# One transformer layer with expert choice: the output projection split in two halves, root refinement and scaling one pair later, row sums behind the masks in the last batch

## The chip, the core and the metric

One core of one Trainium2 chip. The metric is the device time of one execution in microseconds; of the kernel before it was measured three times, and the median counts. One further execution was taken with the hardware profiler. Matrix products run on TensorE (PE; its weight loads are PEld), elementwise work and reductions on VectorE (DVE), activations and copies on ScalarE (ACT), some elementwise work on GpSimd (POOL); SyncE (SP) issues most transfers.

## The reference, cut to what matters

The input is x, 16 batches of 256 rows of 256 numbers, and a condition per batch. All is float32.

```
h   = layernorm(x) * g + b + (silu(cond) @ W_ada.T + b_ada)
qkv = h @ Wqkv.T                       # 16 heads of 64
q,k = layernorm over each head of 64, times gain, plus bias
o   = softmax(q @ k.T / 8) @ v         # per batch and head
x   = x + o @ Wout.T                   # the output projection
gate = softmax(x @ Wgate.T)            # 8 experts
each expert takes its 512 best tokens of all 4096: layernorm, two linear
layers with gelu between, times the gate value, added to the token's row
```

## The kernel before

**Entries and steps.** The attention part runs through `over_batches` (L172): an entry −1 that prepares, entries 0 to 15, one per batch, and an entry 16 that finishes. Entries 2 to 13 are a hardware loop, the others are written out. `cur`, `nxt` and `prv` say whether the entry attends its own batch, projects q, k and v of the next, and finishes the one before. An entry has eight steps (`hp`), one per pair of heads, and every engine has its own in-order program of them, tied by semaphores. Behind the entries the experts are chosen and run (`phase23_*`), which the change touches in one count.

**One step on TensorE** (L1381 on), in this order: transposes of q and k of the next pair (L1398, into `pq`); a chunk of q, k or v for the coming group of pairs (`chunk`, six matmuls of 512 columns, lines L488 to L490 of the helper `three_passes`); the product of probabilities and V of the pair before (L1420, into `av`); that pair's row sums (`ones` times `prob_sum`, L1424, also into `av`); the masks, which write minus the row maximum into `sc` (L1436); the scores of this pair (L1445); rough scores of the next pair for its row maximum (L1458, into `mx`); a second chunk. Steps 2 and 6 have no chunks. The masks need the row maxima `m`, the scores also the low half `qk_lo`.

**What the others do in a step.** ScalarE evacuates the transposes (L1060 to L1066), takes logarithm and exponential of the row sums for their inverse (L1087, L1089), then the exponential of the scores (L1093), then the high half of the divided output (`o_hi`, L1098). GpSimd adds the two halves of the probabilities (`prob_sum`, L980), makes `qk_lo` (L987) and the low half `o_lo` (L992). VectorE divides (three instructions, L1250 to L1254), sums squares of the chunks (L1215) and takes the maxima (L1269), in that order. PE's product of a pair waits for the division of the pair before (`divided`).

**Scaling of q and k.** For each group of four pairs the inverse roots are guessed on ScalarE (`power_guess`, L1006), refined by four small operations on GpSimd (`refine`, L941) and applied on VectorE (`normalise`, L1180, four `times_rstd` of 128x512, L894). For the group of pairs 4 to 7 all three stand in step 0 (in entry 0 `refine` stands in step 1, ahead of `qk_lo`).

**Output projection.** Step 0 of an entry ends with the whole projection of the batch before: 2 row tiles by 8 pairs by 3 passes, 48 matmuls of 256 columns (L1475 on). It waits for `o_lo` of pairs 0 to 6, and in the first tile for that of pair 7 just before it is used. In step 1 VectorE subtracts the result from the residual row `xr_sb` into `tok` (L1233; the division leaves its result with the sign turned), in step 2 it takes statistics of `tok`, in step 3 those of the next input; in step 6 PE transposes `tok` and forms the gate's logits.

**Banks.** Chunks, projection, transposes and logits alternate between the two PSUM banks `ch`. `batch_slots` lists who uses one in each entry and who reads it, `make_counts` derives parity and the wait that frees the bank two uses later:

```
        if prv:
            out += [(0, 2, "wout", "dve"), (6, 0, "tokT", "act"), (6, 1, "gate", "dve")]
```

**SyncE** stores `tok` and reloads `xr_sb` when VectorE has read the projection.

## Time and profile before

| | us |
|---|---|
| median of 3 runs | 1189.99 |
| lowest, highest | 1188.55, 1192.36 |
| the profiled execution, its own time | 1187.28 |
| its span, first to last instruction | 1185.4 |
| PE busy in the span | 1089.6 |

Two microseconds of the profiled execution lie around its span. In the profile "busy" is the time in which an engine works at something; for PE the ends are modelled, so the distance from one matmul's start to the next is the better measure of its pace. An idle time is put down to what ended it. Attention takes the span to about 901 us, the choice of tokens goes to about 983 us, the experts take the rest.

### The profile page before, as it was taken

The page shows a single profiled execution, that of the slowest core. Times are in us where ns is not written, and L with a number is a line of the kernel's source. Part 1 is how long each engine was busy: PE and PEld are TensorE (multiplying, and loading weights), DVE is VectorE, ACT ScalarE, POOL GpSimd, SP SyncE. Part 2 cuts the span into 40 slices and gives each one's busy share as a digit, 9 for nine tenths or more (in the row PEclk, how much of TensorE's full clock was granted, in tenths as well). Part 3 has the DMA queues.
Part 4 walks back from the last instruction along what each step waited for, and adds up shares of the span by engine and source line. Part 5 has one row for each costly group of instructions (what it writes and reads, how often), then busy time and mean ns, then how long its engine had stood idle before and what let it go on. Part 6 is the DMA issues. An engine that isn't in the chain of part 4 may idle for free.

```text
span 1185.4 us, 24714 instructions
## 1 busy us (share of the span) xinstructions
PE 1089.6 (92%) x8379; PEld 844.3 (71%) x8379; DVE 794.8 (67%) x1620; ACT 773.8 (65%) x1460; POOL 555.3 (47%) x597
## 2 busy tenths in 40 slices
PE   6899999999999999999999999999994138999996
PEld 6667777777777777777777777777753037989995
DVE  5686667666675767666666757676655885777773
ACT  5787877868687878778687878787772104445541
POOL 2454545546464545455464645454561003454332
PEclk9999999999999999999999999999997557999998
DMA  4000000010100000000101000000004212554322
GB/s 177 19 10 19 19 19 19 18 35 0 35 18 18 18 18 18 18 18 18 35 0 35 18 18 18 18 9 19 11 19 160 50 36 92 150 153 126 107 27 28
DMA packets 31774, 48.62 MB, mean 41 GB/s; under 512 B 7920, under 2 KB 28528, under 8 KB 30448
## 3 DMA queue, kind: packets, MB, share of 16 engines
q1 hardware_dynamic: 25584, 39.49, 10.2%
q0 software_dynamic: 6144, 8.52, 4.0%
q8 instruction: 28, 0.46, 0.2%
q14 instruction: 18, 0.15, 0.0%
HBM read 35.29 MB, written 12.71 MB: 40 GB/s over the span
## 4 chain that ended last, share of the span: by engine, by line
PE 86%; DVE 7%; issue 2%; POOL 2%; ACT 2%; DMA 1%; SPq 0%; DVEq 0%; POOLq 0%; ACTq 0%
PE ch L488 14%; PE ch L490 12%; PE ch L489 12%; PE av L1420 10%; PE sc L1445 9%; PE sc L1436 6%; PE pq L1398 5%; PE av L1424 5%; PE mx L1458 2%; DVE hit L765 2%; PE sc L488 1%; PE sc L490 1%; PE sc L489 1%; PE ch L1472 1%; PE ch L1378 1%
## 5 line engine op out<-in xcount | busy, mean ns | idle before, releaser
L987 POOL TENSOR_TENSOR qk_lo<-qkT,qk_hi 128x512 fp32r<-128x512 f32 x128 | 169.8, 1327 | 259.7 <-ACT qk_hi L1066 236.6
L980 POOL TENSOR_TENSOR prob_sum<-prob 128x512 f32<-128x512 f32 x128 | 165.0, 1289 | 81.7 <-ACT prob L1093 81.4
L1250 DVE TENSOR_TENSOR av<-av,rec 128x256 f32<-128x256 f32 x128 | 55.2, 431 | 205.9 <-ACT rec L1089 200.9
L488 PE MATMUL ch<-w_hi,hT_lo 128*128 128x512 f32 x384 | 170.5, 444 | 1.0 <-DVE hT_lo L1243 1.0
L1093 ACT ACTIVATE prob<-sc 128x1024 f32<-128x1024 f32 x128 | 130.8, 1022 | 38.2 <-PE sc L1445 38.2
L1269 DVE TENSOR_REDUCE m<-mx 128x4 bf16<-128x1024 f32 x128 | 155.6, 1216 | 0.0
L490 PE MATMUL ch<-w_hi,hT_hi 128*128 128x512 f32 x384 | 151.7, 395 | 0.0
L489 PE MATMUL ch<-w_lo,hT_hi 128*128 128x512 f32 x384 | 151.5, 395 | 0.0
L1420 PE MATMUL av<-prob,V 128*64 128x256 f32 x1024 | 139.6, 394 | 6.3 <-DVE oT L1254 4.3
L894 DVE TENSOR_TENSOR qn<-raw,rstd 128x512 f32<-128x512 f32 x128 | 118.1, 981 | 32.6 <-POOL rstd L956 32.6
L992 POOL TENSOR_TENSOR o_lo<-oT,o_hi 128x256 fp32r<-128x256 f32 x128 | 100.6, 786 | 26.1 <-ACT o_hi L1098 26.1
L1420 PEld LDWEIGHTS av<-prob,V 128*64 128x64 f32 x1024 | 62.6, 136 | 64.5 <-issue 43.1
L1060 ACT ACTIVATE qkT<-pq,vec 128x256 f32<-128x256 f32 x128 | 71.7, 560 | 54.5 <-PE pq L1398 54.5
L590 POOL DMA_INDIRECT out<-yout,index x32 | 52.3, 1633 | 104.5 <-DVE yout L887 98.1
L641 ACT ACTIVATE yT<-ch,b_sb 128x512 f32<-128x512 f32 x62 | 42.6, 688 | 89.4 <-PE ch L490 80.1
L1215 DVE TENSOR_REDUCE ssum<-sq 128x8 f32<-128x512 f32 x128 | 87.1, 681 | 15.6 <-ACT sq L1045 13.8
L488 PEld LDWEIGHTS ch<-w_hi,hT_lo 128*128 128x128 f32 x384 | 72.2, 188 | 22.9 <-DVE hT_lo L1243 1.2
L1066 ACT ACTIVATE qk_hi<-qkT 128x512 fp32r<-128x512 f32 x128 | 80.7, 630 | 11.6
L1043 ACT ACTIVATE raw<-ch 128x512 f32<-128x512 f32 x128 | 75.1, 587 | 16.8 <-PE ch L490 15.9
L1445 PE MATMUL sc<-qk_hi,qk_lo 64*128 64x256 f32 x512 | 85.6, 330 | 0.0
L490 PEld LDWEIGHTS ch<-w_hi,hT_hi 128*128 128x128 f32 x384 | 72.3, 188 | 18.0
L1424 PE MATMUL av<-prob_sum,ones 128*64 128x256 f32 x512 | 77.8, 382 | 1.9 <-POOL prob_sum L980 1.9
(214 smaller groups left out, 2797.3 us busy)
## 6 DMA issues: line engine op xcount, KB each, us to landing
fcw<-experts SPq DMA_DIRECT2D x8, 2048.0 KB
x_sb<-x SPq DMA_DIRECT2D x16, 256.0 KB, 2.7
xr_sb<-x SPq DMA_DIRECT2D x16, 256.0 KB, 2.7
out<-tok SPq DMA_DIRECT2D x16, 256.0 KB, 2.2
rows_dram<-xh SPq DMA_DIRECT2D x16, 256.0 KB, 2.2
prob<-w_qk SPq DMA_DIRECT2D x2, 512.0 KB, 6.8
qn<-w_qk SPq DMA_DIRECT2D x2, 512.0 KB, 7.2
V<-w_vT SPq DMA_DIRECT2D x2, 512.0 KB, 7.3
```

Of the source, the lines that this page charges most:

```text
L488: nc.tensor.matmul(psum, l_lo, r_hi, start=first, stop=False)
L489: nc.tensor.matmul(psum, l_hi, r_lo, start=False, stop=False)
L490: return nc.tensor.matmul(psum, l_hi, r_hi, start=False, stop=last)
L894: return nc.vector.tensor_tensor(qn[par][:, c, :].rearrange("p (h d) -> p h d", d=HD), raw[:, c, :].rearrange("p (h d) -> p h d", d=HD), r ...
L980: nc.gpsimd.tensor_tensor(prob_sum[(hp - 1) % 2][:, :, :], pr[:, :, 0, :], pr[:, :, 1, :], ALU.add).then_inc(prob_summed, 1)
L987: nc.gpsimd.tensor_tensor(qk_lo[par][:, :], qkT[par][:, :], qk_hi[par][:, :].bitcast(F32), ALU.subtract).then_inc(lo_ready, 1)
L992: nc.gpsimd.tensor_tensor(o_lo[:, pair, :], oT[pair % 2][:, :], o_hi[:, pair, :].bitcast(F32), ALU.subtract).then_inc(o_split, 1)
L1093: nc.scalar.activation(prob[hp % 2][:, :], sc[:, :], ACT.Exp, scale=HD ** -0.5).then_inc(prob_ready, 1)
L1269: nc.vector.tensor_reduce(m[(hp + 1) % 2][:, :], mx[:, :].rearrange("p (a j) -> p a j", a=4), AX.X, ALU.max).then_inc(max_ready, 1)
L1420: nc.tensor.matmul(av[hh * HD:(hh + 1) * HD, 0:N], V[gpar][:, jt, i * P + hh * HD:i * P + (hh + 1) * HD], prob[(hp - 1) % 2][:, at:at + N] ...
L1424: ins = nc.tensor.matmul(av[hh * HD:(hh + 1) * HD, N:2 * N], ones[:, :], prob_sum[(hp - 1) % 2][:, hh, :], start=True, stop=True)
L1445: ins = nc.tensor.matmul(sc[:, at:at + N], k_part[par][rows, keys], q_part[par][rows, 0:N], start=False, stop=(k_part is qk_hi and q_part ...
```

## The change

The projection is made in two halves. Pairs 0 to 3 of a batch are projected at the end of step 6 of its own entry, and VectorE subtracts the result from `xr_sb` in place at the start of step 7. Pairs 4 to 7 are projected at the end of step 2 of the next entry, and VectorE makes `tok` from that at the start of step 3. Both row statistics of VectorE now stand at the end of step 3. The logits share the bank of the transposed `tok`, so that an entry still has sixteen uses of a bank. `power_guess`, `refine` and `normalise` of pairs 4 to 7 move from step 0 to step 1, `refine` behind `qk_lo`. In entry 15, steps 3 to 7, the row sums stand behind the masks. Entry 0 has a first half and no second, entry 16 a second and no first.

```diff
--- before.py
+++ after.py
@@ -68,7 +68,9 @@
     cur, nxt, prv = 0 <= b < B, b + 1 < B, 1 <= b <= B
     out = [(hp, pos, name, "act") for (hp, pos), (name, _) in CHUNKS.items() if (cur if hp < 2 else nxt)]
     if prv:
-out += [(0, 2, "wout", "dve"), (6, 0, "tokT", "act"), (6, 1, "gate", "dve")]
+out += [(2, 0, "wout_second", "dve"), (6, 0, "tokT", "act"), (6, 1, "gate", "dve")]
+    if cur:
+out += [(6, 2, "wout_first", "dve")]
     if nxt:
 out += [(1, 2, "xT", "act")]
     return sorted(out)
@@ -89,7 +91,10 @@
     key = (hp, pos)
     hit("slot", b, key)
     hit(who, b, key)
-    slots.append((b, key, who))
+    if name == "gate":
+        slots[-1] = (b, (6, 0), who, key)
+    else:
+        slots.append((b, key, who, key))
     if name in ("q", "k"):
         hit("chunk", b, key)
 for hp, live in ((0, cur or b < 0), (4, nxt or prv)):
@@ -98,12 +103,11 @@
 for kind, live in (("x_loaded", nxt), ("xr_loaded", cur), ("tok_stored", prv)):
     if live:
         hit(kind, b, 0)
-    for n, (b, key, who) in enumerate(slots):
-table["bank", b, key] = n % 2
-table["index", b, key] = n
+    for n, (b, key, who, last) in enumerate(slots):
+table["bank", b, key] = table["bank", b, last] = n % 2
 if n >= 2:
-    pb, pkey, pwho = slots[n - 2]
-    table["free", b, key] = (pwho, table[pwho, pb, pkey])
+    pb, _, pwho, plast = slots[n - 2]
+    table["free", b, key] = (pwho, table[pwho, pb, plast])
     return table
@@ -738,7 +742,7 @@
-    dve.wait_ge(dve_read, 2 * B)
+    dve.wait_ge(dve_read, 3 * B)
@@ -903,7 +907,7 @@
             sp.dma_start(x_sb[:, :, :], x[bass.ds(b + 2, 1)].rearrange("o (t p) d -> p (o t) d", p=P)
                          if not isinstance(b, int) else x[b + 2].rearrange("(t p) d -> p t d", p=P)).then_inc(x_in, 16)
         if prv:
-            need(dve_read, through("dve", b, (0, 2)))
+            need(dve_read, through("dve", b, (2, 0)))
@@ -978,8 +982,6 @@
...
-            if isinstance(b, int) and b == 0 and hp == 1:
-                refine(b, 0)
             if (cur and nxt) or (cur and hp < UNITS - 1) or (nxt and hp == UNITS - 1):
                 need(hi_ready, u + 2)
@@ -990,7 +992,7 @@
...
-            if hp == 0 and cur and not (isinstance(b, int) and b == 0):
+            if hp == 1 and cur:
                 refine(b, 0)
             if hp == 5 and (nxt or prv) and not (isinstance(b, int) and b == B):
                 refine(b, 4)
@@ -1071,6 +1073,8 @@
                 value_weights_high()
             if isinstance(b, int) and b < 0 and hp == 5:
                 weights_high(1, 0)
+            if hp == 1 and cur:
+                power_guess(b, 0)
             if hp == 5 and (nxt or prv) and not (isinstance(b, int) and b == B):
                 power_guess(b, 4)
             if isinstance(b, int) and b < 0 and hp == 5:
@@ -1094,12 +1098,12 @@
             if (cur and hp > 0) or (hp == 0 and prv):
                 need(divided, u)
                 if hp == 1 and prv:
-                    need(slot_filled, through("slot", b, (0, 2)))
+                    need(slot_filled, through("slot", b - 1, (6, 2)))
+                if hp == 5 and prv:
+                    need(slot_filled, through("slot", b, (2, 0)))
             if live:
                 chunk(b, hp, 1)
-            if hp == 0 and cur:
-                power_guess(b, 0)
             if hp == 1 and nxt:
                 need(slot_filled, through("slot", b, (1, 2)))
@@ -1221,17 +1225,23 @@
     need(rstd_ready, 1)
     input_rows(rstd[1])
+    def flat_rows(t):
+        return t[:, :, :].rearrange("p t d -> p (t d)")
+
     def batch(b, cur, nxt, prv):
         last_entry = isinstance(b, int) and b == B
         for hp in range(UNITS):
             u = b * UNITS + hp
-            if hp == 1 and prv:
-                need(slot_filled, through("slot", b, (0, 2)))
-                need(xr_in, b * 16)
+            if hp == 3 and prv:
+                need(slot_filled, through("slot", b, (2, 0)))
+                need(dve_read, through("dve", b - 1, (6, 2)))
                 need(tok_out, (b - 1) * 16)
                 need(xh2_ready, b - 1)
-                nc.vector.tensor_tensor(tok[:, :, :].rearrange("p t d -> p (t d)"), xr_sb[:, :, :].rearrange("p t d -> p (t d)"),
-                                        ch[slot_bank(b, (0, 2))][:, :], ALU.subtract).then_inc(dve_read, 1)
+                nc.vector.tensor_tensor(flat_rows(tok), flat_rows(xr_sb), ch[slot_bank(b, (2, 0))][:, :], ALU.subtract).then_inc(dve_read, 1)
+            if hp == 7 and cur:
+                need(slot_filled, through("slot", b, (6, 2)))
+                need(xr_in, (b + 1) * 16)
+                nc.vector.tensor_tensor(flat_rows(xr_sb), flat_rows(xr_sb), ch[slot_bank(b, (6, 2))][:, :], ALU.subtract).then_inc(dve_read, 1)
@@ -1252,9 +1262,6 @@
-            if hp == 3 and has_second(b):
-                need(x_in, (b + 3) * 16)
-                row_stats(x_sb, 0)
             if hp in (0, 3, 4, 7) and (cur if hp < 2 else nxt):
                 head_sums(b, hp, 0)
             if hp == 6 and prv:
@@ -1284,13 +1291,15 @@
                 else:
                     need(slot_filled, through("slot", -1, (1, 2)))
                 input_rows(rstd[0])
-            if hp == 2 and prv and not last_entry:
-
-                need(dve_read, through("dve", b, (0, 2)))
-                row_stats(tok, 2)
-            if hp == 2 and last_entry:
-                need(dve_read, through("dve", b, (0, 2)))
-                last_stats()
+            if hp == 3 and has_second(b):
+                need(x_in, (b + 3) * 16)
+                row_stats(x_sb, 0)
+            if hp == 3 and prv:
+                need(dve_read, through("dve", b, (2, 0)))
+                if last_entry:
+                    last_stats()
+                else:
+                    row_stats(tok, 2)
             if (hp == 0 and cur) or (hp == 4 and (nxt or prv) and not last_entry):
                 need(rstd_ready, through("newton", b, hp) - 1)
@@ -1300,7 +1309,7 @@
                     need(chunk_summed, through("chunk", b, (hp, 1)))
-            if hp == 0 and cur:
+            if hp == 1 and cur:
                 normalise(b, 0)
             if isinstance(b, int) and b == 0:
                 split_wout(hp)
@@ -1371,6 +1380,22 @@
                                w_hi[:, c, col:col + GW], w_lo[:, c, col:col + GW], c == 0, c == DC - 1)
         ins.then_inc(slot_filled, 1)
+    def project(bank, pairs):
+
+        for t in range(TT):
+            for pair in pairs:
+                ins = three_passes(bank[:, t * D:(t + 1) * D], o_hi[:, pair, t * P:(t + 1) * P], o_lo[:, pair, t * P:(t + 1) * P],
+                                   wo_hi[:, pair, :], wo_lo[:, pair, :], pair % GU == 0, pair % GU == GU - 1)
+        ins.then_inc(slot_filled, 1)
+
+    def row_sums(u, hp):
+
+        need(prob_summed, u)
+        for hh in range(2):
+            ins = nc.tensor.matmul(av[hh * HD:(hh + 1) * HD, N:2 * N], ones[:, :], prob_sum[(hp - 1) % 2][:, hh, :],
+                                   start=True, stop=True)
+        ins.then_inc(attended, 1)
+
@@ -1383,6 +1408,7 @@
             u = b * UNITS + hp
             ahead = (cur and nxt) or (cur and hp < UNITS - 1) or (nxt and hp == UNITS - 1)
             npar = (hp + 1) % 2
+            bare = cur and not nxt and hp > 2
             if isinstance(b, int) and b < 0 and hp == 2:
                 centre_weights(0, 1)
             if isinstance(b, int) and b < 0 and hp == 5:
@@ -1401,7 +1427,7 @@
                 chunk(b, hp, 0)
             if hp == 6 and prv:
                 bank = take_bank(b, (6, 0))
-                need(dve_read, through("dve", b, (0, 2)))
+                need(dve_read, through("dve", b, (2, 0)))
                 transposed(bank, tok)
             if (cur and hp > 0) or (hp == 0 and prv):
@@ -1419,11 +1445,8 @@
...
-                need(prob_summed, u)
-                for hh in range(2):
-                    ins = nc.tensor.matmul(av[hh * HD:(hh + 1) * HD, N:2 * N], ones[:, :], prob_sum[(hp - 1) % 2][:, hh, :],
-                                           start=True, stop=True)
-                ins.then_inc(attended, 1)
+                if not bare:
+                    row_sums(u, hp)
             if cur:
                 need(prob_ready, u)
@@ -1436,6 +1459,8 @@
...
+                if bare:
+                    row_sums(u, hp)
                 for jt in range(TT):
                     keys = slice(N + jt * P, N + (jt + 1) * P)
@@ -1465,25 +1490,25 @@
                 need(xh_ready, b + 2)
                 transposed(bank, xh)
             if hp == 6 and prv:
-                bank = take_bank(b, (6, 1))
+                bank = ch[slot_bank(b, (6, 1))]
                 need(act_read, through("act", b, (6, 0)))
...
-            if hp == 0 and prv:
-                bank = take_bank(b, (0, 2))
-                need(o_split, u - 1)
+            if hp == 2 and prv:
+                bank = take_bank(b, (2, 0))
+                need(o_split, u - 2)
                 if isinstance(b, int) and b == 1:
                     need(wo_ready, 2 * UNITS)
-                for t in range(TT):
-                    for pair in range(UNITS):
-                        if t == 0 and pair == UNITS - 1:
-                            need(o_split, u)
-                        ins = three_passes(bank[:, t * D:(t + 1) * D], o_hi[:, pair, t * P:(t + 1) * P], o_lo[:, pair, t * P:(t + 1) * P],
-                                           wo_hi[:, pair, :], wo_lo[:, pair, :], pair == 0, pair == UNITS - 1)
-                ins.then_inc(slot_filled, 1)
+                project(bank, range(GU, UNITS))
+            if hp == 6 and cur:
+                bank = take_bank(b, (6, 2))
+                need(o_split, u - 2)
+                if isinstance(b, int) and b == 0:
+                    need(wo_ready, UNITS)
+                project(bank, range(GU))
     over_batches(pe, batch)
     phase23_tensor(pe)
```

(Indentation is cut by eight columns.)

## Rows read from the trace of the kernel before

**Rows 1.** The page: TensorE's granted clock, in tenths, in 40 slices of the span.

```profile
PEclk9999999999999999999999999999997557999998
```

**Rows 2.** Windows by engine: stretch, length, busy us (instructions) per engine, granted clock, DMA.

```profile
48.40:51.70 3.30, 3.30 (x16) 1.69 (x16) 2.73 (x5) 3.21 (x8) 0.00 (x0) 0.55 0.00 0
80.00:134.40 54.40, 54.40 (x428) 40.62 (x426) 37.10 (x76) 42.62 (x87) 28.78 (x33) 1.00 0.06 16
```

**Rows 3.** Timeline of entry 0, steps 1 to 5: start, length, instruction, [idle before].

```profile
41.73 4.66 DVE L894 TENSOR_TENSOR qn<-raw,rstd 128x512 f32<-128x512 f32 x4 [1.90 <-POOL rstd L956]
...
42.78 0.42 ACT L1089 ACTIVATE rec<-log_sum 128x256 f32<-128x256 f32 x1
...
44.54 0.60 PE L1398 MATMUL pq<-con,qn 128*128 128x128 f32 x4
...
46.97 0.42 DVE L1250 TENSOR_TENSOR av<-av,rec 128x256 f32<-128x256 f32 x1
...
48.40 1.98 PE L1420 MATMUL av<-prob,V 128*64 128x256 f32 x8 [3.26 <-DVE oT L1254]
...
50.59 0.69 DVE L1243 TENSOR_TENSOR hT_lo<-hT,hT_hi 128x512 fp32r<-128x512 f32 x1
...
53.33 0.48 PE L488 MATMUL ch<-w_hi,hT_lo 128*128 128x512 f32 x1
...
73.08 2.83 DVE L894 TENSOR_TENSOR qn<-raw,rstd 128x512 f32<-128x512 f32 x4
```

**Rows 4.** Timeline of a middle entry, step 0: around the output projection.

```profile
580.04 0.74 POOL L992 TENSOR_TENSOR o_lo<-oT,o_hi 128x256 fp32r<-128x256 f32 x1 [1.56 <-ACT o_hi L1098]
580.08 0.28 PE L488 MATMUL ch<-wo_hi,o_lo 128*128 128x256 f32 x1
...
585.84 0.60 PE L1398 MATMUL pq<-con,qn 128*128 128x128 f32 x4
...
587.77 1.08 PE L1420 MATMUL av<-prob,V 128*64 128x256 f32 x8
```

**Rows 5.** Timeline of the last full entry, steps 2 and 3, TensorE.

```profile
867.63 0.40 PE L1458 MATMUL mx<-qk_hi 64*128 64x256 f32 x4
...
868.98 1.08 PE L1420 MATMUL av<-prob,V 128*64 128x256 f32 x8 [0.36 <-ACT prob L1093]
```

**Rows 6.** Timeline of the last full entry, one period of steps 4 and 5, all engines.

```profile
872.41 1.02 ACT L1093 ACTIVATE prob<-sc 128x1024 f32<-128x1024 f32 x1 [0.62 <-PE sc L1445]
...
873.49 1.08 PE L1420 MATMUL av<-prob,V 128*64 128x256 f32 x8 [0.29 <-ACT prob L1093]
873.51 1.28 POOL L980 TENSOR_TENSOR prob_sum<-prob 128x512 f32<-128x512 f32 x1 [0.55 <-ACT prob L1093]
...
874.84 0.65 PE L1424 MATMUL av<-prob_sum,ones 128*64 128x256 f32 x4 [0.27 <-POOL prob_sum L980]
875.43 0.61 PE L1436 MATMUL sc<-neg_ident,m 128*128 128x256 bf16 x4
...
875.97 0.39 PE L1445 MATMUL sc<-qk_hi,qk_lo 64*128 64x256 f32 x2
...
876.99 1.02 ACT L1093 ACTIVATE prob<-sc 128x1024 f32<-128x1024 f32 x1 [0.62 <-PE sc L1445]
...
877.68 1.22 DVE L1269 TENSOR_REDUCE m<-mx 128x4 bf16<-128x1024 f32 x1
```

**Rows 7.** Timeline of the last full entry, steps 6 and 7.

```profile
886.65 1.02 ACT L1093 ACTIVATE prob<-sc 128x1024 f32<-128x1024 f32 x1 [0.62 <-PE sc L1445]
886.78 1.06 PE L1472 MATMUL ch<-wg_sb,tokT 128*128 128x8 f32 x8
...
891.22 1.02 ACT L1093 ACTIVATE prob<-sc 128x1024 f32<-128x1024 f32 x1 [0.61 <-PE sc L1445]
```

**Rows 8.** Timeline after the last pair: the last projection and what follows.

```profile
893.64 0.65 PE L1424 MATMUL av<-prob_sum,ones 128*64 128x256 f32 x4 [0.26 <-POOL prob_sum L980]
...
897.87 0.39 PE L488 MATMUL ch<-wo_hi,o_lo 128*128 128x256 f32 x1 [0.70 <-POOL o_lo L992]
```

## The prediction

> **What bounds the kernel now.** I read the page first. TensorE is busy 92% of the span, and its granted clock is at the full 2.4 GHz through most of the attention part [rows 1]. Then the windows, one batch long: in each of the fourteen that follow one another from 80.0 to 841.6 us PE is busy for all 54.40 us [rows 2], where the first of them stands. Busy ends are modelled, so I checked starts in the timeline: the 48 projection matmuls run from 580.08 to 585.84, 0.12 us each, without a hole [rows 4]. Entries 1 to 14 are bound by the number of matmuls alone; moving work there between steps is worth nothing unless it makes PE wait. Waits of PE on the others are left at two places. In entry 0 PE stands 3.26 us before a product at 48.40, because the division of pair 0 on VectorE comes behind the four scalings of q and k [rows 3]; and a part of the following stretch has half clock [rows 2]. In entry 15, steps 3 to 7, there are no chunks to fill PE, and it goes round a chain of ScalarE, GpSimd and PE in 4.58 us [rows 6].
>
> **The middle entries (1 to 14).** PE issues the same 48 matmuls in each, 24 behind the rough scores of step 2 and 24 behind the logits of step 6. What can differ is the seam between kinds of matmuls. A seam costs at most some 0.1 us (four masks take 0.54 us from 875.43 to 875.97, four projection matmuls 0.48 [rows 4, 6]); one is added in step 2 and none in step 6, where transposes followed before too. I take 0; ends -0.05 and +0.1 us per entry, -0.7 and +1.4 us in all. Step 0 loses the 5.76 us of projection that covered the others. Its cover is needed least by V's product; nearest to a wait are the row sums of pair 0. GpSimd ends the last `o_lo` at 580.78 and needs 1.28 us for `prob_sum` [rows 4, 6]: 582.1. PE would start the product of pair 0 at 580.08 + 1.93 = 582.0 (transposes and chunk, as from 585.84 to 587.77 [rows 4]), and the row sums 0.9 us later. Slack 0.8 us, cost 0. `refine` and `power_guess` in step 1 wait for a variance that step 0 already made, so ScalarE and GpSimd stand no longer than before. `normalise` ends step 1 on VectorE; behind it are the split of hT and a division, needed a chunk and a half projection later. The extra load of step 3 on VectorE (subtraction of `tok`, two statistics) lies at its ends, behind the maximum of pair 4. SyncE's store of `tok` and reload of `xr_sb` start two steps later; the reload has four steps until step 7.
>
> **Entry 0, the scaling moved.** VectorE's work from 41.73 to the end of `hT_lo` at 51.28 is: scalings 4.66 us, split of a weight 0.6, division and maximum, another split, hT [rows 3]. After, the division of pair 0 comes first, when its reciprocal is there, at 43.2 or up to 0.7 us earlier because the two root guesses leave ScalarE's path; the split is done while waiting (-0.6), and the scalings should take the 2.83 us of the later row rather than 4.66 (-1.83), as GpSimd's `prob_sum` is then over [rows 3]. End: 51.28 + 1.5 - 0.6 - 1.83 = 50.35, or 49.65. PE gets V's product of pair 1 without a wait at 45.1 and would be ready for the first chunk of step 3 at 45.1 + (53.33 - 48.40) - 1.5 (lost to the clock, 45% of 3.30 us [rows 2]) = 48.6. So that chunk waits for hT and starts at about 50.0 instead of 53.33: **-3.3 us**. Ends: -1.5, if the scalings again take 4.66, and -4.7, if hT is no limit.
>
> **Entry 0, the first half** of batch 0 at step 6 is new on a dense PE: 24 x 0.12 = **+2.9 us**. Nothing hides it.
>
> **Entry 15.** Step 0 loses 48 matmuls, -5.76. Step 2 gains 24: 2.88 and 0.1 for the seam. The rough scores end at 867.96, so V's product of pair 2 starts at 867.96 + 2.98 + 0.4 (transposes) = 871.3 instead of 868.98 [rows 5]. Masks now stand next (0.91 + 0.54), then the row sums at 872.8, and the exponential of pair 3 follows 1.61 us behind their start (from 874.84 to 876.99 less the masks' 0.54 [rows 6]): 874.4, 2.0 later than 872.41. Steps 4 to 6 are the place of the third part of the change. One would count that the masks leave the chain. They do, but another chain closes: row sums, logarithm, division, maximum of the next pair, masks, row sums. From a row-sum start at 874.84 the maximum ends at 877.68 + 1.22 = 878.90; with 0.05 for the signal and 0.54 for the masks the next row sums start 4.65 us later, against 4.58 now [rows 6]. So +0.1 in two periods, and in step 6, where GpSimd's refinement holds `prob_sum`, I take no change. Ends: -0.44 per period, if only the product and masks (1.08 + 0.91 + 0.54 + 1.61 = 4.14) bind; +0.1 per period for the added seam. Step 7: behind the exponential at 886.65 the logits are issued at 886.78 and take 1.0, then 24 matmuls 2.98, product and masks 1.45, row sums and scores 1.61: 7.15 us to the next exponential, now 4.57 [rows 7]: +2.6. The sum of entry 15: -5.76 + 2.0 + 0.1 + 2.6 = **-1.1 us**.
>
> **Entry 16.** The last `o_lo` sets the start of the projection at 897.87. Then 27 matmuls were left, now 24: **-0.4 us** [rows 8]. The 21 that ran ahead of it were hidden; PE now stands idle instead.
>
> **Sum.** -3.3 + 2.9 - 1.1 - 0.4 = -1.9 us. Against the profiled execution (span 1185.4, time 1187.28) that gives 1185.4 us; it ran 2.7 us under the median of the runs, so for the median 1190.0 - 1.9 = **1188.1 us**. About 0.3% (3.6 us) is what a measurement of this kernel can tell from no change.
>
> Two rules of the Trainium skill speak against the change. The page "TensorEngine Tiling (Array Packing)", section Key Properties, says that a change of tiling mode drains TensorE; masks between two products of 64 output columns add such a change in steps 3 to 7. The trace agrees as far as the seams of some 0.1 us go; by the rule alone entry 15 would be 0.5 us slower. The other stands with the first rival.
>
> **Rivals.** (a) *The clock falls in the tail.* In entry 0 PE stood 3.26 us and the stretch behind had a granted clock of 0.55 on average, between the levels of 1.2 and 2.4 GHz [rows 2, 3]. After the change PE has nothing between the last row sums (0.65 us from 893.64) and 897.87, 3.6 us [rows 8]. If the clock falls there, the 24 matmuls lose what that stretch lost, 1.5 us: -0.4 in all, 1189.6. For it speaks the length of the gap, against it that entry 15's earlier gaps of about 0.3 us in 4.6 left the clock full [rows 6]. Chance 0.3. The page "TensorE: Matmul & The Clock Gate", section "Why this matters for your kernels", advises against just such idle gaps between bursts, for the clock drops behind them.
> (b) *Both gains in full.* VectorE's loop does not bind (4.14 us in three periods, -1.4) and entry 0 loses its whole wait (-4.7): -4.7 in all, 1185.3, faster. Against it stands the order of VectorE's program. Chance 0.2.
> (c) *A wait in every entry, slower.* In step 1 the row sums of pair 0 come to wait for GpSimd, once the projection is gone from before them. It decides at 0.8 us of lateness of `prob_sum`; each further 0.1 us costs 1.4 us over fourteen entries. At 1.2 us late it is +5.6, 1193.7. For it: GpSimd's work is done late in step 0. Against: it ends there at 580.78 in steady order, and the slack holds without the refinement [rows 4]. Chance 0.06.
> (d) *Entry 0 gains nothing to speak of*, as the scalings only delay hT instead: -1.5 in place of -3.3, near 1189.9. Chance 0.06.
>
> **Chances and range.** The forecast has 0.38. It, (a) and (d) lie within 0.3%: 0.74. Faster by over 0.3% is (b), 0.2; slower (c), 0.06. For the range: entry 0 at -4.7 rather than -3.3, three short periods -1.4, seams -0.7 give 1184.6; entry 0 at -1.5, the clock +1.5, seams +1.4 give 1192.8, which leaves out most of (c). I take 1184.6 to 1192.8.
>
> **What would show it.** Middle windows still 54.40 us, PE full. In entry 0 no half clock, the product of pair 1 at about 45, the first chunk of step 3 at about 50. In entry 15 periods of exponentials of about 4.65 us with PE's masks waiting for the maximum of VectorE, and 7.1 us in step 7. At the end 24 matmuls behind `o_lo`. Periods near 4.1 would make the VectorE loop wrong; a wait of PE on GpSimd's `prob_sum` in the middle entries would make the forecast wrong as a whole.

## The result and the profile after

The changed kernel ran at 1191.98 us (median of 22 runs, 1187.69 to 1193.67), the kernel before beside it at 1188.44 us (22 runs, 1185.93 to 1192.36). The ratio is 1.0023, with a 95% interval of 1.0013 to 1.0033: slower by 1.5 to 3.9 us, where 1.9 us less had been forecast. The profiled execution took 1190.2 us, its span 1188.4 against 1185.4. So the two profiles also differ by 3.0 us, and that is the sum to be explained.

The page of the changed kernel, TensorE's granted clock in 40 slices (answers to [rows 1]):

```profile
PEclk9999999999999999999999999999996567999998
```

Windows of the changed kernel (columns as in [rows 2]: stretch, length, busy us of PE, PEld, DVE, ACT, POOL, granted clock, DMA share, GB/s):

```profile
51.97:55.40 3.43, 3.43 (x16) 1.61 (x14) 1.87 (x4) 2.93 (x6) 1.23 (x2) 0.50 0.00 0
80.00:134.40 54.40, 54.40 (x425) 40.56 (x424) 38.26 (x77) 42.08 (x84) 29.01 (x32) 1.00 0.07 21
896.00:905.00 9.00, 5.46 (x24) 5.20 (x24) 1.21 (x4) 1.07 (x3) 0.73 (x1) 0.64 0.01 3
```

PE is as full in the middle as before. A stretch at half clock is still there in entry 0, some 4 us later than before, and at the end of attention there is a stretch at 0.64 on average that the kernel before did not have. The change of time, step by step, can be read off ScalarE's 128 exponentials (`prob<-sc`), one for each pair, whose starts in the timelines of both kernels mark the same point of the work:

| mark | before, us | after, us | after - before | gained since the mark above | forecast for it |
|---|---|---|---|---|---|
| entry 0, pair 0 | 36.22 | 36.68 | +0.46 | +0.46 | ahead of any edit |
| entry 0, pair 3 | 57.93 | 57.22 | -0.71 | -1.17 | -3.3 |
| entry 1, pair 0 | 89.09 | 90.15 | +1.06 | +1.77 | +2.9 |
| entry 15, pair 0 | 850.35 | 852.68 | +2.33 | +1.27 | 0 |
| entry 15, pair 7 | 891.22 | 892.73 | +1.51 | -0.82 | -1.1 |
| start of the last `tok` (DVE) | 901.40 | 904.97 | +3.57 | +2.06 | -0.4 |
| end of the span | 1185.4 | 1188.4 | +3.0 | -0.57 | 0 |

From the first mark to the last `tok` that is +3.1 us, against the forecast's -1.9; the +0.46 and the -0.57 lie outside of what was edited. They are spread between executions: in the twelve profiles of this document the first mark lies between 35.5 and 38.5 us, and what follows the last `tok` takes 283.0 to 286.0 us, with no relation to the edits. The middle entries and entry 15, in contrast, repeat within some 0.1 us wherever the program is the same. Now the rows behind the two largest differences.

**The tail.** Timeline of the changed kernel after its last pair, TensorE; below it its list of waits, PE alone (engine, line, releaser: us in total, times, longest):

```profile
899.47 0.55 PE L492 MATMUL ch<-wo_hi,o_lo 128*128 128x256 f32 x1 [3.67 <-POOL o_lo L994]
...
903.88 0.41 PE L494 MATMUL ch<-wo_hi,o_hi 128*128 128x256 f32 x1
904.09 0.41 PE L492 MATMUL ch<-wo_hi,o_lo 128*128 128x256 f32 x1
```

```profile
PE ch L492 <- POOL o_lo L994: 3.7, 1, 3.7
```

The wait of 0.70 us in [rows 8] has become 3.67. The matmuls behind it start 0.213 us apart (24 of them, the last at 904.52), where those of a middle entry start 0.12 apart [rows 4]. Three fewer matmuls stand behind `o_lo`, and yet it takes 2.06 us longer to `tok`.

**Entry 0.** Timeline of the changed kernel, steps 1 to 3, VectorE, then GpSimd, then TensorE (answers to [rows 3]):

```profile
44.89 2.79 DVE L898 TENSOR_TENSOR qn<-raw,rstd 128x512 f32<-128x512 f32 x4
47.60 0.28 DVE L1159 CAST wo_hi<-wo_sb 128x256 fp32r<-128x256 f32 x1
47.91 0.42 DVE L1161 TENSOR_TENSOR wo_lo<-wo_sb,wo_hi 128x256 fp32r<-128x256 f32 x1
48.26 1.51 DVE L1252 CAST hT_hi<-hT 128x512 fp32r<-128x512 f32 x1
49.80 1.09 DVE L1253 TENSOR_TENSOR hT_lo<-hT,hT_hi 128x512 fp32r<-128x512 f32 x1
...
47.99 1.49 POOL L989 TENSOR_TENSOR qk_lo<-qkT,qk_hi 128x512 fp32r<-128x512 f32 x1 [2.67 <-ACT qk_hi L1068]
49.44 0.90 POOL L994 TENSOR_TENSOR o_lo<-oT,o_hi 128x256 fp32r<-128x256 f32 x1
...
45.53 1.08 PE L1446 MATMUL av<-prob,V 128*64 128x256 f32 x8
...
51.04 0.47 PE L492 MATMUL ch<-w_hi,hT_lo 128*128 128x512 f32 x1 [1.71 <-DVE hT_lo L1253]
```

The four scalings are back to 2.79 us and the product of pair 1 starts at 45.53 instead of 48.40 [rows 3], both as forecast. The cast of hT however takes 1.51 us and ends only after GpSimd's `qk_lo`, beside which it lies, and `hT_lo` goes on past GpSimd's `o_lo`. Then PE runs at half clock from 51.97: from the chunk to the next exponential it is 57.22 - 51.04 = 6.18 us, before 57.93 - 53.33 = 4.60.

**Entry 15.** One period of the changed kernel, all engines (answers to [rows 6]):

```profile
871.21 1.03 ACT L1097 ACTIVATE prob<-sc 128x1024 f32<-128x1024 f32 x1
...
872.44 1.21 DVE L1276 TENSOR_REDUCE m<-mx 128x4 bf16<-128x1024 f32 x1
872.67 1.08 PE L1446 MATMUL av<-prob,V 128*64 128x256 f32 x8 [0.68 <-DVE oT L1264]
873.76 0.60 PE L1459 MATMUL sc<-neg_ident,m 128*128 128x256 bf16 x4
874.28 0.65 PE L1395 MATMUL av<-prob_sum,ones 128*64 128x256 f32 x4
...
875.89 1.03 ACT L1097 ACTIVATE prob<-sc 128x1024 f32<-128x1024 f32 x1
...
877.15 1.21 DVE L1276 TENSOR_REDUCE m<-mx 128x4 bf16<-128x1024 f32 x1
...
878.99 0.65 PE L1395 MATMUL av<-prob_sum,ones 128*64 128x256 f32 x4
```

Row sums to row sums is 4.71 us (874.28 to 878.99), 1.61 us behind their start the next exponential begins: the loop by way of VectorE's division and maximum that was forecast at 4.65.

### The profile page after: what moved, and what is told of

Its sections match the earlier page's. It is cut to its first block, busy times and chain, and to the rows that moved or that the text cites. A ratio compares the mean times of both kernels' runs of the same rounds, so it can differ in the third digit from the quotient of the medians.

```text
span 1188.4 us, 24797 instructions
## 1 busy us (share of the span) xinstructions
PE 1093.4 (92%) x8379; PEld 847.6 (71%) x8379; DVE 794.3 (67%) x1636; ACT 780.4 (66%) x1460; POOL 560.3 (47%) x597
## 4 chain that ended last, share of the span: by engine, by line
PE 89%; DVE 7%; ACT 1%; issue 1%; DMA 1%; POOL 1%; SPq 0%; DVEq 0%; ACTq 0%; POOLq 0%
PE ch L492 15%; PE ch L494 12%; PE ch L493 12%; PE av L1446 11%; PE sc L1470 9%; PE sc L1459 6%; PE av L1395 5%; PE pq L1424 5%; PE mx L1483 2%; DVE hit L769 2%; PE ch L1497 1%; PE sc L492 1%; PE sc L494 1%; PE sc L493 1%; PE ch L1403 1%
## 5 line engine op out<-in xcount | busy, mean ns | idle before, releaser
L989 POOL TENSOR_TENSOR qk_lo<-qkT,qk_hi 128x512 fp32r<-128x512 f32 x128 | 173.9, 1359 | 290.4 <-ACT qk_hi L1068 270.2
L898 DVE TENSOR_TENSOR qn<-raw,rstd 128x512 f32<-128x512 f32 x128 | 105.5, 881 | 0.0
L492 PE MATMUL ch<-wo_hi,o_lo 128*128 128x256 f32 x256 | 76.5, 299 | 3.7 <-POOL o_lo L994 3.7
```

The source lines that it names most:

```text
L492: nc.tensor.matmul(psum, l_lo, r_hi, start=first, stop=False)
L898: return nc.vector.tensor_tensor(qn[par][:, c, :].rearrange("p (h d) -> p h d", d=HD), raw[:, c, :].rearrange("p (h d) -> p h d", d=HD), r ...
L989: nc.gpsimd.tensor_tensor(qk_lo[par][:, :], qkT[par][:, :], qk_hi[par][:, :].bitcast(F32), ALU.subtract).then_inc(lo_ready, 1)
```

## The experiments

Ten kernels were run. The theory after the result: the change puts PE work where PE is full (step 6) and takes it from where PE then stands idle, and the granted clock falls behind the new gap; in entry 0 VectorE's queue ahead of the first chunk eats most of the gain. The rivals: the rows behind masks are what costs, or a seam or a wait in each middle entry.

### e1_rows_in_place

```diff
-                    bare = cur and not nxt and hp > 2
+                    bare = False
```

> The changed kernel with the row sums of entry 15 ahead of the masks again. Theory (VectorE's loop binds): the periods between the exponentials of steps 3 to 5, 4.68 and 4.71 us in the changed kernel, go back to 4.58, that of step 6 stays near 4.9 to 5.1; the whole is 0 to 0.3 us faster. Rival (the masks left the chain and the periods have another cause): they get longer, towards 5.1, as the masks' 0.54 us come back onto the chain.

Measured: 1192.32 us, ratio to the kernel before 1.0020 (1.0005 to 1.0036); the change itself has 1.0023. The periods of steps 3 to 7 were 6.64, 4.57, 4.58, 5.08 and 7.09 us, against 6.79, 4.68, 4.71, 4.90 and 7.24 in the changed kernel: 0.36 us less in the five. The third part of the change costs a little and is not the cause. The tail from the last exponential to `tok` took 11.11 us here, 12.24 in the changed kernel and 10.18 in the kernel before, although the wait for the last `o_lo` is the same as in the changed kernel (3.66 and 3.67 us).

### e7_rows_alone

```diff
-                        need(prob_summed, u)
...
+                        if not (cur and not nxt and hp > 2):
+                            row_sums(u, hp)
...
+                        if cur and not nxt and hp > 2:
+                            row_sums(u, hp)
```

(On the kernel before, with the new helper and nothing else of the change.)

> The kernel before with only the row sums behind the masks in steps 3 to 7 of entry 15. Theory: periods of 4.65 to 4.71 us instead of 4.58, the whole 0 to 0.4 us slower. Rival: periods of 4.1 to 4.2 us, the whole 1.5 us faster.

Measured: 1188.91 us, ratio 1.0004 (0.9986 to 1.0022). Timeline, one period:

```profile
873.22 1.08 PE L1428 MATMUL av<-prob,V 128*64 128x256 f32 x8 [0.71 <-DVE oT L1254]
874.31 0.60 PE L1441 MATMUL sc<-neg_ident,m 128*128 128x256 bf16 x4
874.84 0.65 PE L1378 MATMUL av<-prob_sum,ones 128*64 128x256 f32 x4
```

The periods were 4.37, 4.70, 4.68, 4.89 and 4.76 us, before 4.57, 4.58, 4.58, 5.08 and 4.57: 23.40 against 23.38 in all. PE's product now waits for VectorE's `oT`, where in [rows 6] it waited for ScalarE's `prob`. The masks left one chain and the time went into the other, so that the edit alone moves nothing.

### e2_filled_tail

```diff
                         bank = take_bank(b, (2, 0))
+                        if isinstance(b, int) and b == B:
+                            for n in range(28):
+                                nc.tensor.matmul(mx[:, 0:D], wo_hi[:, 0, 0:P], wo_hi[:, 1, :], start=True, stop=True)
                         need(o_split, u - 2)
```

> The changed kernel with 28 matmuls of 256 columns into an unused bank while TensorE would stand idle ahead of the last projection (their result is not used). Theory (the idle gap of 3.67 us lowers the clock): the 24 matmuls of the last projection start 0.12 us apart instead of 0.21, the subtraction into tok starts about 10.0 us behind the last exponential's start instead of 12.24, and the median is 2 to 3.5 us lower than the changed kernel's 1191.98. Rival (the tail is slow because nothing runs ahead of the last o_lo, or the low clock is there whatever precedes): no change, or slower by the time of the added matmuls.

Measured: 1189.49 us, ratio 0.9996 (0.9982 to 1.0011); the changed kernel's was 1.0023. Windows and timeline of the tail:

```profile
896.00:905.00 9.00, 7.87 (x62) 6.87 (x60) 2.76 (x9) 1.38 (x4) 1.29 (x2) 1.00 0.01 2
```

```profile
900.17 0.38 PE L492 MATMUL ch<-wo_hi,o_lo 128*128 128x256 f32 x1
...
900.63 0.28 PE L492 MATMUL ch<-wo_hi,o_lo 128*128 128x256 f32 x1
900.75 0.28 PE L493 MATMUL ch<-wo_lo,o_hi 128*128 128x256 f32 x1
```

28 matmuls whose result nobody reads make the kernel faster: by 2.4 us in the tail of this profile, by 3.2 us if the two ratios are compared (each is known to 1 to 2 us). The clock is 1.00 where it was 0.64, the projection's matmuls start 0.12 us apart again, and from the last exponential to `tok` it is 9.84 us instead of 12.24. Nothing but PE's activity in the gap was changed; the cause of the longer tail is the granted clock, and the cause of that is the gap. The Trainium skill says the same: "TensorE: Matmul & The Clock Gate", section "Why this matters for your kernels", advises against idle gaps between bursts, for the clock drops behind them; behind the gap of 3.67 us here it did.

### e3_nine_ahead

```diff
...
                     for pair in pairs:
+                        if last and t == 0 and pair == UNITS - 1:
+                            need(o_split, last)
...
-                        need(o_split, u - 2)
+                        final = isinstance(b, int) and b == B
+                        need(o_split, u - 3 if final else u - 2)
...
+                        project(bank, range(GU, UNITS), u - 2 if final else None)
```

> The changed kernel, in entry 16 the nine matmuls of pairs 4 to 6 of the first row tile run ahead of the wait for the last o_lo. Theory: 15 matmuls remain behind it; at full clock tok starts 10.18 - 12 x 0.12 = 8.7 us behind the last exponential's start, at half clock 10.2; nine matmuls fill 1.1 us of the gap of 3.67, so the clock may hold or not. Rival (the idle gap has no part in it): 12.24 less 9 x 0.21 = 10.3, in every run at half clock.

Measured: 1188.37 us, ratio 0.9983 (0.9967 to 0.9999).

```profile
900.98 0.38 PE L492 MATMUL ch<-wo_hi,o_lo 128*128 128x256 f32 x1 [2.15 <-POOL o_lo L994]
```

The nine matmuls of pairs 4 to 6 that need nothing of the last `o_lo` run in the gap, which is cut to 2.15 us. Exponential to `tok` is 8.74 us, 3.5 less than in the changed kernel: 15 matmuls behind `o_lo` instead of 24 (1.1 us), and the clock is full until 906.7. This is work of the kernel itself, and it replaces the filler with profit. The change had dropped it: the loop of the kernel before waited for the last `o_lo` only ahead of pair 7.

### e4_splits_later

```diff
-                        split_wout(hp)
+                        for pair in {0: (0,), 3: (1,), 4: (2,), 5: (3,), 6: (4, 5), 7: (6, 7)}.get(hp, ()):
+                            split_wout(pair)
```

> The changed kernel, with the splits of the output weights moved out of steps 1 and 2 of entry 0 into steps 3 to 7. Theory (VectorE reaches the cast of hT only when GpSimd has begun qk_lo and waits it out, 1.51 us for an operation of 0.43, and the clock falls behind the wait): without the split of 0.7 us ahead of it the cast starts before GpSimd and takes 0.43; the first chunk of step 3 starts at about 48.9 us instead of 51.04, the clock stays full in entry 0, and the median is 2 to 4 us lower. Rival (the cast is slow for its own reasons, or VectorE has too much work anyway): the chunk gains 0.7 us at most.

Measured: 1194.43 us, ratio 1.0035 (1.0020 to 1.0050). The gain came where it was looked for and was paid back later in the same entry. The period of pair 3's exponential in entry 0 is 6.15 us instead of 8.67, with no low clock there. But the period of pair 7's is 13.80 instead of 8.04. Windows, then timeline of step 6:

```profile
77.00:83.80 6.80, 5.92 (x28) 5.95 (x29) 5.27 (x12) 0.42 (x1) 0.45 (x1) 0.50 0.15 41
```

```profile
77.88 0.55 PE L492 MATMUL ch<-wo_hi,o_lo 128*128 128x256 f32 x1 [3.05 <-DVE wo_lo L1161]
```

The first half needs the weights of pairs 0 to 3, and the last of them is now split behind the scalings of step 5. PE waits 3.05 us for it and then works at half clock: a second gap of this size with the same end.

### e5_root_alone

```diff
-                    if hp == 0 and cur and not (isinstance(b, int) and b == 0):
+                    if hp == 1 and cur:
                         refine(b, 0)
...
+                    if hp == 1 and cur:
+                        power_guess(b, 0)
...
-                    if hp == 0 and cur:
+                    if hp == 1 and cur:
                         normalise(b, 0)
```

(On the kernel before; the projection stays whole in step 0.)

> The kernel before with only root guess, refinement and scaling of pairs 4 to 7 moved to step 1. Theory: entry 0 loses about 1.2 us up to the exponential of pair 3, as in the changed kernel; the middle windows keep 54.38 us; the whole is 1 to 2 us faster than before. Rival (the move costs ScalarE or GpSimd a wait in each entry): entries longer than 54.40 us.

Measured: 1193.62 us, ratio 1.0031 (1.0014 to 1.0048). Entry 0 gains 2.6 us up to pair 3's exponential, and no half clock is left there; it gives back 1.15 us by the first exponential of entry 1, where PE waits 0.85 us for a scaling and 1.39 us for a division on VectorE in step 7. Timeline of entry 0, PE, then windows of the stretch behind:

```profile
50.33 0.47 PE L488 MATMUL ch<-w_hi,hT_lo 128*128 128x512 f32 x1 [1.71 <-DVE hT_lo L1241]
```

```profile
51.26:54.69 3.43, 3.43 (x32) 2.11 (x32) 1.87 (x4) 3.19 (x7) 1.22 (x2) 1.00 0.00 0
```

The wait of 1.71 us is the same as in the changed kernel, the chunk starts 14.36 us behind the first exponential in both, and yet the clock stays full here: from the chunk to the exponential it is 4.74 us, in the changed kernel 6.18.

The loss is in the middle: entries 2 to 13 take 54.73 us from exponential to exponential, before 54.38, entry 1 takes 55.19 and entry 14 55.26; over the fourteen that is +6.0 us. Timeline, step 3 of a middle entry, PE and GpSimd:

```profile
491.02 1.08 PE L1418 MATMUL av<-prob,V 128*64 128x256 f32 x8
492.23 0.65 PE L1422 MATMUL av<-prob_sum,ones 128*64 128x256 f32 x4
...
488.48 1.78 POOL L985 TENSOR_TENSOR qk_lo<-qkT,qk_hi 128x512 fp32r<-128x512 f32 x1 [2.79 <-ACT qk_hi L1064]
...
490.92 1.26 POOL L980 TENSOR_TENSOR prob_sum<-prob 128x512 f32<-128x512 f32 x1
```

From the product to the row sums it is 1.21 us instead of the 0.91 of a full PE: `prob_sum` ends at 492.18, late because `qk_lo` took 1.78 us beside VectorE's split of hT. In the changed kernel the half projection of step 2 lies ahead of this place, and PE has no such wait in its middle entries; that the one covers the other is read from the order of the program and was not tested.

### e6_halves_alone

```diff
+                    if isinstance(b, int) and b == 0 and hp == 1:
+                        refine(b, 0)
...
-                    if hp == 1 and cur:
+                    if hp == 0 and cur and not (isinstance(b, int) and b == 0):
                         refine(b, 0)
...
-                    if hp == 1 and cur:
+                    if hp == 0 and cur:
                         normalise(b, 0)
...
-                    bare = cur and not nxt and hp > 2
+                    bare = False
```

(On the changed kernel, `power_guess` back in step 0 likewise.)

> The changed kernel with root refinement and scaling back in step 0 and the row sums ahead of the masks: the two halves alone. Theory: each middle entry is 0.09 us longer than before for its seams, entry 0 bears 24 matmuls more (2.9 us, less what fills a wait), entry 15 gives back about 1 us, the tail loses 2 us to the clock: 3 to 5 us slower than before. Rival (the halves are free on a dense TensorE and the slowdown is of the scaling's move): within 1 us of before.

Measured: 1255.57 us, ratio 1.0561 (1.0538 to 1.0584), the largest effect of all. Waits of PE, then the timeline of step 1 of a middle entry, PE and GpSimd:

```profile
PE av L1397 <- POOL prob_sum L984: 38.0, 19, 2.4
```

```profile
506.43 0.68 PE L1397 MATMUL av<-prob_sum,ones 128*64 128x256 f32 x4 [2.44 <-POOL prob_sum L984]
507.05 1.04 PE L1461 MATMUL sc<-neg_ident,m 128*128 128x256 bf16 x4
...
500.95 0.74 POOL L996 TENSOR_TENSOR o_lo<-oT,o_hi 128x256 fp32r<-128x256 f32 x1 [1.56 <-ACT o_hi L1104]
...
503.89 0.25 POOL L951 TENSOR_TENSOR na<-guess 128x36 f32<-128x36 f32 x1 [2.21 <-ACT guess L1018]
...
505.11 1.27 POOL L984 TENSOR_TENSOR prob_sum<-prob 128x512 f32<-128x512 f32 x1
```

GpSimd sits 2.21 us before the refinement for ScalarE's guess, `prob_sum` is queued behind it, and PE waits for that in every entry: 34.1 us over entries 1 to 14. In the kernel before, the whole projection in step 0 covered the refinement. The masks then take 1.04 us instead of 0.61: the clock falls here, as in 8 of the 14 entries. An entry at full clock is 57.9 us long against 54.47 in the changed kernel (2.65 us more in the period with the wait, 0.93 in the next), one with a low stretch 58.6 to 59.9; entries 1 to 14 are together 57.3 us longer than in the kernel before. So the two first parts of the change need each other. Alone they cost about 4 us (the root) and 66 us (the halves); together the middle entries lose 0.09 us each.

### e8_half_in_gap

```diff
...
+                    if hp == 0 and isinstance(b, int) and b == B:
+                        bank = take_bank(B - 1, (6, 2))
+                        need(o_split, B * UNITS - UNITS + GU)
+                        project(bank, range(GU))
-                    if hp == 6 and cur:
+                    if hp == 6 and cur and not (isinstance(b, int) and b == B - 1):
```

(VectorE's subtraction of this half moves from step 7 of entry 15 to step 1 of entry 16; that part of the edit is left out here.)

> The changed kernel, with the last batch's first half moved again: from step 6 of entry 15, where nothing hides its 24 matmuls, to behind the last row sums of entry 16, where PE otherwise stands 3.7 us for the last o_lo; its subtraction on VectorE goes along. Theory (the loss is one of cover: PE work put where PE is full, and taken from where PE then stands idle and the clock falls): the last period of exponentials goes from 7.2 to 4.6 us, and from the last exponential to tok it is 9.8 us (as in the run with filler) instead of 12.2, with no low clock before tok: 5.0 us less than the changed kernel, some 1 to 2 us less than the kernel before. Rival (the clock falls for another reason, or the 24 matmuls in the gap are late themselves and push the second half back by more than they fill): the last period shortens, but the tail stays at 11 us or more: about 3 us less than the changed kernel, no different from the kernel before.

Measured: 1186.25 us (lowest 1183.85; 12 runs), ratio 0.9980 (0.9967 to 0.9993). One execution took 2158.36 us and is left out of the ratio.

```profile
898.47 0.35 PE L492 MATMUL ch<-wo_hi,o_lo 128*128 128x256 f32 x1 [0.60 <-POOL o_lo L994]
```

The last period is 4.77 us instead of 7.24, and from the last exponential to `tok` it is 9.87, with 24 more matmuls in it and no low clock before the choice of tokens. Both are the theory's numbers (4.6 and 9.8). By the ratios it is 1188.2 x (1.0023 - 0.9980) = 5.1 us better than the changed kernel, where 5.0 was expected; in the profiles, between the first exponential and the last `tok`, it is 4.9. The rival is out: the 24 matmuls fit into the gap.

### e9_splits_when_due

```diff
-                        split_wout(hp)
+                        for pair in {0: (0,), 3: (1, 2), 4: (3,), 6: (4,), 7: (5, 6, 7)}.get(hp, ()):
+                            split_wout(pair)
```

> The changed kernel, with VectorE's splits of the output weight in entry 0 at steps 0, 3, 3, 4, 6, 7, 7, 7 instead of one in each step: none in steps 1 and 2, but those of pairs 0 to 3, which the first half needs, done by step 4. Theory (entry 0 gained 1.2 us and not 3.3 because VectorE's split and the casts of hT stand ahead of the first chunk of step 3, and the late weight splits of the earlier run cost its step 6): period of the exponential of pair 3 of entry 0 6.2 us instead of 8.7, no low clock near 52 us, and the period of step 6 stays at 8.0 us: 2.5 us less than the changed kernel, about 1188. Rival (VectorE has no slack at all up to step 6, so that what is taken out of steps 1 and 2 comes back later, as in the earlier run): the sum over the periods of entry 0 up to the exponential 1.0 is unchanged within 0.5 us, time as the changed kernel.

Measured: 1188.79 us, ratio 1.0003 (0.9992 to 1.0015), 2.4 us under the changed kernel by the ratios. Timeline of entry 0, VectorE, then GpSimd, then TensorE:

```profile
47.00 0.41 DVE L1252 CAST hT_hi<-hT 128x512 fp32r<-128x512 f32 x1
47.45 1.78 DVE L1253 TENSOR_TENSOR hT_lo<-hT,hT_hi 128x512 fp32r<-128x512 f32 x1
...
47.40 1.28 POOL L989 TENSOR_TENSOR qk_lo<-qkT,qk_hi 128x512 fp32r<-128x512 f32 x1 [2.67 <-ACT qk_hi L1068]
48.64 1.18 POOL L994 TENSOR_TENSOR o_lo<-oT,o_hi 128x256 fp32r<-128x256 f32 x1
...
49.37 0.47 PE L492 MATMUL ch<-w_hi,hT_lo 128*128 128x512 f32 x1 [0.64 <-DVE hT_lo L1253]
```

Without the split of a weight ahead of it the cast starts before GpSimd's `qk_lo` and takes 0.41 us; PE waits 0.64 us instead of 1.71, and the clock stays full. Pair 3's period is 6.16 us instead of 8.67. The later splits cost little: from the first exponential of entry 0 to that of entry 1 it is 51.17 us, against 53.47 in the changed kernel. The theory's numbers came (6.2, 8.0 and about 1188), so the rival, that VectorE has no slack up to step 6, is out.

### e10_all

The edits of e1, e3, e8 and e9 together.

> The changed kernel with row sums in their old place (0.4 us), the weight splits when due (2.5), the last batch's first half in the gap of entry 16 (5.0), and nine matmuls of the second half ahead of the wait for the last o_lo (1.1). Theory (the gains are at different places of the program and add): 8 to 9 us less than the changed kernel, about 1183, and 6 us less than the kernel before. Rival (the gap is filled once only, and nine matmuls ahead find it closed, or the gain in entry 0 doesn't come): 5 to 6 us less than the changed kernel, about 1186.

Measured: 1181.54 us (6 runs, 1180.65 to 1185.30), ratio 0.9951 (0.9934 to 0.9967) to the kernel before, which had 1188.16 us. That is faster than both kernels: by 4 to 8 us than the kernel before, and by the ratios 8.6 us than the changed one, where 8 to 9 had been expected. The gains add. From the last exponential to `tok` it is 9.07 us, and PE waits no longer for the last `o_lo`.

## Why the prediction was wrong

The measured time lies in the range and in the class that had the highest chance, within 0.3%; the direction was wrong, 1.9 us less against about 3 more. That the time lies in the range is no merit of the forecast: the upper end, 2.8 us above the kernel before, was put together from a small gain in entry 0, the clock in the tail and seams in each entry, and these three are what came. Step by step:

**Entry 16, -0.4: the step that failed most; +2.06 came.** "Then 27 matmuls were left, now 24 ... PE now stands idle instead" priced the idle time at nothing. The three matmuls less are worth what was forecast: with the gap filled (e2) the tail is 9.84 us against 10.18, -0.34. The term left out is the clock behind the gap, 12.24 - 9.84 = +2.40 us. Rival (a) named the mechanism and had 0.3; it should have been the forecast, as the gap of 3.6 us was longer than the 3.26 us of [rows 3], behind which half clock stood in the same trace. Its price, 1.5 us from a stretch at 0.55 and 3.3 us long, was too low for this profile, where the low stretch lasted 6.8 us and all 24 matmuls ran at half clock: (0.213 - 0.12) x 24 = 2.2 us. In e1, e6 and e9 the low stretch lasted 3.4 us, and the tail was 1.3 to 1.5 us longer than e2's. What spoke against it, gaps of 0.3 us in 4.6, was a different size of gap. e2 shows the cause by filling the gap, e3 and e8 by filling it with work.

**Entry 0, -3.3; -1.17 came.** The order of VectorE's program, the 2.79 us for the scalings and the product at 45.5 were right, and so nearly was the chunk: 51.04 less the 0.46 us by which this profile starts later is 50.6, against "about 50.0". What failed is "1.5 (lost to the clock ...)", taken off as if the half clock went with the wait. PE was busy for 3.81 of the 5.52 us from 46.45 to 51.97 (windows), with 1.71 us of waiting for `hT_lo`, and the half clock came behind that instead: 1.6 us more from chunk to exponential. e9 and e4 cut the wait to 0.64 us, and the low clock goes with it. The wait alone does not decide, however: e1, e2, e3 and e8 lost the clock behind the same wait as the changed kernel, e5 did not, and what differs is not known. With e5 between them the two losses can be told apart: against e9 the period of pair 3 is 1.07 us longer in e5, by the late chunk, and another 1.44 in the changed kernel, by the clock. The remaining 0.6 us of the miss are the chunk's: the cast of hT took 1.51 instead of 0.43 us and the subtraction 1.09 instead of 0.69, and the division of pair 0, 1.1 us earlier than the forecast's 43.2 (42.55 less 0.46), made good most of that.

**Entry 0's first half, +2.9; +1.77 came.** "Nothing hides it" overlooked a wait in the trace of before: the product of pair 6, in step 7, stood 1.01 us for the division on VectorE. The 24 matmuls (2.98 us) cover that now; 0.2 us of the difference is not accounted for. e6 has the first half without the scaling's move and shows +1.75 in the same stretch. e5 has the move without the first half and shows +1.15, from PE's waits for VectorE in step 7, so the move has a cost here that the 24 matmuls cover as well. The line of the trace of the kernel before, timeline of step 7 of entry 0:

```profile
79.42 1.08 PE L1420 MATMUL av<-prob,V 128*64 128x256 f32 x8 [1.01 <-DVE oT L1254]
```

**The middle entries, 0; +1.27 came**, at the upper end (+1.4). An entry takes 54.47 us, before 54.38 (means over entries 2 to 13). PE has no wait; the 48 matmuls took 5.76 us and now take 2.96 and 2.98, the transposes together 0.09 less: a seam of 0.1 us, as the upper bound had it. This is read from the rows; no run tests the seam by itself. The rest of this step was right, the slack of `prob_sum` in step 0 included. Timeline of the changed kernel, GpSimd and TensorE, step 1 of a middle entry:

```profile
473.69 1.30 POOL L984 TENSOR_TENSOR prob_sum<-prob 128x512 f32<-128x512 f32 x1
...
474.98 1.08 PE L1446 MATMUL av<-prob,V 128*64 128x256 f32 x8
475.89 0.60 PE L1395 MATMUL av<-prob_sum,ones 128*64 128x256 f32 x4
```

`prob_sum` ends at 474.99, 0.9 us ahead of the row sums; 0.8 was forecast. Rival (c) did not come. e6 shows that it was the right thing to fear: with the refinement left in step 0 its mechanism costs 38 us of waits and half clock in 8 of the 14 entries.

**Entry 15, -1.1; -0.82 came.** Periods of 4.68 and 4.71 us for "about 4.65", 7.24 for 7.15, and the period of step 3 grew by 2.2 us for the forecast 2.0; that of step 6, where no change was taken, fell by 0.2. Rival (b), whose condition was that VectorE's loop does not bind, is out by e7 as well. The profile shows the first of its two gains (short periods) absent, and of the second (entry 0's whole wait, -4.7) only 1.17 us.

That the terms fit the cause and not only the sum is shown by e8, e9 and e10, which undo the losses one by one: -5.1, -2.4 and, all together, -8.6 us against the changed kernel by the ratios. The profiles, read from the first exponential to the last `tok`, say the same: 868.3 us in the changed kernel, 863.4 in e8, 865.0 in e9 (2.3 of its gain in entry 0, the rest in a shorter tail) and 860.0 in e10, where the kernel before has 865.2.

Three things stay open. The low clock behind the gap of 3.7 us did not last equally long in each profile: 6.8 us in the changed kernel and in e4, 3.4 us in e1, e6 and e9, and from the last exponential to `tok` it was 12.24 and 12.23 us, and 11.11 to 11.32, with the same wait. Why the clock stayed full in entry 0 of e5 behind a wait that cost it elsewhere is open as well; neither was tried. And the execution of 2158 us was seen once and not explained.

## What to carry to other kernels

When a block of matmuls is moved, price both ends: the place that it goes to (is PE full there?) and the place that it leaves, where a gap of some 3 us costs twice, once as idle time and once at half clock behind it. If a stretch at half clock stands behind a wait in the trace of before, ask of the new gaps whether they are as long, and do not book the clock's loss as regained while a wait of one or two microseconds is left ahead: in these runs such a wait sometimes cost the clock and sometimes did not. Two edits that look separate may hide each other's costs, so test each alone before keeping or dropping one.

## What was unexpected of the hardware

- **A cast on VectorE waited out a GpSimd operation.** `hT_hi` 128x512 took 1.51 us in the changed kernel, where GpSimd's `qk_lo` had begun first (47.99 to 49.48), and 0.41 us in e9, where `qk_lo` began as it ended. `hT_lo` took 0.69 us with GpSimd idle (kernel before, [rows 3]), 1.09 us begun behind `o_lo` and 1.78 behind `qk_lo`. It goes the other way too: `qk_lo` took 1.78 us instead of 1.28 in e5 and `o_lo` 1.18 instead of 0.74 in e9, when VectorE's work was ahead of them. The page "SBUF — State Buffer" of the Trainium skill, section "Who interferes with whom", has it as an exclusive lock on a pair of ports that both engines use, held for the whole instruction; the starts and ends of these rows fit that. For the time of the kernel: e9's period of pair 3 is 2.51 us shorter than the changed kernel's, 1.07 of it up to the first chunk (from 14.36 to 13.29 us behind the first exponential) and 1.44 by the clock behind it (6.18 to 4.74 us from that chunk to the exponential). A rearrangement of 0.7 us of work on VectorE did both.
- **Useless matmuls gain time.** 28 of them in an idle gap shorten the tail by 2.4 us (e2).
- **A gap of 1.71 us was followed by half clock, too, but not always.** In entry 0 of the changed kernel PE had no longer single wait than that between 46.45 and 51.97 us; in e9, with 4.88 of the same 5.52 us busy instead of 3.81, the clock stayed full. Among the waits read for this document, half clock came behind those of 3.05 us (e4), 3.26 and 3.27 us (entry 0 of the kernel before, e6 and e7) and 3.66 to 3.67 us (the tail of the changed kernel, e1, e4, e6 and e9); in 8 of 14 entries with a wait of about 2.4 us (e6); behind the wait of 1.7 us in entry 0 in five profiles and not in a sixth (e5); and not behind 2.15 us (e3) or 0.64 us (e4, e9, e10).
